# ScalarE instead of VectorE makes the two halves of the scaled incidence matrix, and every queue is ordered anew

## The reference

```python
# layer 0
h = max(layernorm(x), 0)
A_hat = adj + eye; d = A_hat.sum(-1) ** -0.5
x = x + (A_hat * d[:, :, None] * d[:, None, :]) @ (h @ W + b)
# layer 1
h = max(layernorm(x), 0)
H = (adj != 0); w = adj[:, 0, :]              # edge weights: first row of adj
Dn = 1 / (H @ w);  Be = 1 / H.sum(axis=1)     # node and edge degrees
conv(v, W, b) = Dn * (H @ (Be * (H^T @ (v @ W^T)))) + b
g = layernorm(relu(conv(h, W1, b1)), gamma, beta)   # 512 -> 1024
x = x + conv(g, W2, b2) + h                         # 1024 -> 512
```

## Time and profile before

| | |
|---|---|
| median of 3 runs | 1917.77 us |
| profiled execution, its own time | 1915.19 us |
| its span | 1913.3 us |
| TensorE busy | 1881.8 us, 98% |
| VectorE busy | 1661.5 us, 87% |
| ScalarE busy | 1450.5 us, 76% |
| GpSimd busy | 1235.0 us, 65% |
| mean granted TensorE clock | 0.998 |

### The profile page before, as it was taken

The page is one execution under the profiler, slowest core; times in us unless marked ns, Lnnn a source line. Parts: engine busy times, 40 slices in busy tenths (PEclk is TensorE's granted clock), DMA queues, the critical chain, the costliest instruction groups (busy, mean ns, idle before and its releaser), DMA issues.

```text
span 1913.3 us, 37357 instructions
## 1 busy us (share of the span) xinstructions
PE 1881.8 (98%) x10104; PEld 911.1 (48%) x10104; DVE 1661.5 (87%) x3177; ACT 1450.5 (76%) x2726; POOL 1235.0 (65%) x1554
## 2 busy tenths in 40 slices
...
GB/s 231 58 105 96 108 115 90 106 116 84 108 112 90 108 115 90 108 113 91 108 112 91 107 112 91 108 111 90 111 103 98 111 103 99 111 95 99 83 66 78
DMA packets 518736, 197.65 MB, mean 103 GB/s; under 512 B 466816, under 2 KB 483328, under 8 KB 518528
## 3 DMA queue, kind: packets, MB, share of 16 engines
...
...
## 4 chain that ended last, share of the span: by engine, by line
PE 84%; issue 4%; DVE 4%; POOL 2%; DMA 1%; SPq 0%; ACT 0%; DVEq 0%; POOLq 0%
PE ps_u L405 31%; PE ps_e L405 15%; PE ps_x L416 15%; PE ps_z L416 7%; PE ps_y L416 4%; PE ps_y L456 1%; PE ps_y L458 1%; PE ps_y L457 1%; PE ps_t L393 1%; PE ps_t L394 1%; PE ps_t L395 1%; PE ps_e L456 1%; PE ps_e L458 1%; PE ps_e L457 1%; DMA raw_t<-bet_wide 1%
## 5 line engine op out<-in xcount | busy, mean ns | idle before, releaser
L405 PE MATMUL ps_u<-w2h,raw_t 128*128 128x512 f16 x2016 | 476.2, 379 | 0.0
L1506 POOL TENSOR_TENSOR base<-b_all,xh 128x512 f32<-128x512 f32 x128 | 210.9, 1647 | 353.7 <-DVE raw_w L1141 343.8
L405 PEld LDWEIGHTS ps_u<-w2h,raw_t 128*128 128x128 f16 x2016 | 194.6, 98 | 224.3 <-issue 0.8
L1083 DVE SCALAR_TENSOR_TENSOR raw_w<-ps_x,dn,b_all 128x512 f32<-128x512 f32 x192 | 141.9, 739 | 117.3 <-PE ps_x L416 116.9
L405 PE MATMUL ps_u<-w2l,raw_t 128*128 128x512 f16 x1008 | 238.1, 379 | 0.0
L788 ACT ACTIVATE bet_wide<-raw_w 128x1024 f16<-128x1024 f32 x128 | 134.2, 1048 | 78.8 <-DMA raw_t<-bet_wide 75.3
L1498 POOL TENSOR_TENSOR b_all<-x,b_all 128x512 f32<-128x512 f32 x128 | 167.0, 1305 | 16.7 <-DMA b_all<-in_b_dram 7.7
L1556 POOL TENSOR_SCALAR u<-ssq 128x2 f32<-128x2 f32 x64 | 34.1, 532 | 216.9 <-ACT raw_w L773 216.4
L1511 POOL TENSOR_TENSOR base<-base,raw_w 128x512 f32<-128x512 f32 x128 | 166.8, 1303 | 8.0
L779 ACT ACTIVATE raw_w<-raw_w,nm,sc 128x1024 f32<-128x1024 f32 x128 | 151.9, 1232 | 23.3 <-POOL nm L1582 23.3
L1127 DVE TENSOR_TENSOR bet_wide<-raw_w,bet_wide 128x1024 f16<-128x1024 f32 x128 | 158.7, 1240 | 7.2 <-ACT bet_wide L788 3.6
(11 more groups left out here) (178 smaller groups left out, 4901.3 us busy)
## 6 DMA issues: line engine op xcount, KB each, us to landing
x_t<-in_x_dram SPq DMA_DIRECT2D x128, 256.0 KB, 2.9
out_dram<-raw_w SPq DMA_DIRECT2D x128, 256.0 KB, 2.5
...
raw_t<-bet_wide SPq DMA_TRANSPOSE x256, 3.3
...
h0T_hi<-h_hi SPq DMA_TRANSPOSE x128, 2.5
h0T_lo<-h_lo SPq DMA_TRANSPOSE x128, 2.4
...
```

What stands on the lines that cost most here:

```text
L405: mm = pe.matmul(ps, t[:, j * 128:(j + 1) * 128], w[:, j, :], start=(n == 0 and j == 0), stop=(n == 2 and j == blocks - 1))
L1083: return dve.scalar_tensor_tensor(out=z, in0=bank[:, :], scalar=dn1[:, p % 2, j:j + 1], in1=z if row is None else row[:, cols], op0=ALU.mu ...
L1506: pool.tensor_tensor(base[:, g % 6, :], x1b[:, :], xh[:, g % 2, :], ALU.add).then_inc(s_scr2, 1)
```

## The change

`do_HB_hi` and `do_HB_lo` move from VectorE's queue to ScalarE's. The low half was (H^T x inv) - HB_hi before; now the factor itself is split, `inv_hi = f16(inv)` by ScalarE (`do_invh`) and `inv_lo = inv - inv_hi` by VectorE (`do_invl`), and HB_lo = H^T x inv_lo. `inv_lo` is written into `cm`, `inv_hi` into a spare column of HB. Two semaphores are new, and `do_P` waits for both halves. All five queues are ordered anew: the loop takes two pairs a turn and covers pairs 16 to 51, the fillers are 208 in eleven places in place of 178 in eight, and in the start the weights come in another order.

```diff
-    STEADY_FROM, STEADY_TO = 4, NP - 16
+    STEADY_FROM, STEADY_TO = 16, NP - 12
+        inv_hi, inv_lo = HB[:, 0, :, :, N + 1], cm
@@ SyncE's queue
-            do_ldX(0); do_ldX(1)
+            do_ldX(0); do_ldX(1); do_trA(0)
...
-            do_ldX(2); do_ldX(3); do_ldA(4)
+            do_ldA(3); do_ldX(2); do_ldX(3); do_ldA(4); do_ldA(5); do_trA(2)
             load_weight(1, raw_w1, W1T, range(0, 2))
             load_weight(1, raw_w1, W1T, range(2, 4))
-            do_trA(2); do_tr0h(0); do_tr0h(1); do_ldA(5); do_tr0l(0); do_tr0l(1); do_ldA(6)
+            do_tr0h(0); do_tr0h(1); do_tr0l(0); do_tr0l(1); do_ldA(6); do_ldA(7)
@@ TensorE's queue, start
             def do_P(p):
+                pe.wait_ge(s_hbh, 2 * p + 2)
                 pe.wait_ge(s_hbl, 2 * p + 2)
...
-            keep_busy(14, ps_u)
+            keep_busy(13, ps_u)
             gram_of_weight(0, raw_w0, range(0, 4))
-            keep_busy(18, ps_u)
+            keep_busy(37, ps_u)
             weight_sum(0, gram[:, 0, 0:N + 1])
-            keep_busy(60, ps_x)
+            keep_busy(42, ps_x)
             do_P(0)
+            keep_busy(7, ps_x)
             gram_of_weight(1, raw_w1, range(0, 4))
+            keep_busy(20, ps_x)
+            do_P(1)
+            keep_busy(4, ps_x)
+            weight_sum(1, gram[:, 1, 0:N])
             do_Y0(0); do_Y0(1)
+            beta_row(range(0, 2))
+            beta_row(range(2, 4))
+            do_Z0(0)
+            beta_row(range(4, 6))
+            beta_row(range(6, 8))
             do_Z0(1); do_Y0(2)
             weight_sum(2, wsq[:, 0:KH])
+            do_Y0(3); do_Z0(2)
+            keep_busy(27, ps_x)
+            do_Z0(3)
+            keep_busy(9, ps_x)
+            do_P(2); do_Y0(4); do_T1(0)
+            keep_busy(23, ps_x)
+            do_T1(1); do_Z0(4)
+            keep_busy(7, ps_x)
+            do_Y0(5); do_T1(2)
+            keep_busy(19, ps_x)
+            do_M1(0); do_M2(0); do_Z0(5); do_P(3); do_M6(0); do_M5(0); do_M7(0); do_T1(3); do_Y0(6); do_M3(0)
@@ TensorE's queue, loop
-            for k in range(STEADY_FROM, STEADY_TO):
-                do_M1(k); do_Y0(2 * k + 5); do_U(2 * k - 3); do_M6(k); do_Y2(2 * k - 4); do_P(k+2); do_T1(2 * k + 2)
-                do_M7(k); do_Z0(2 * k + 5); do_M5(k); do_Y0(2 * k + 6); do_Y2(2 * k - 3); do_M3(k); do_M4(k)
-                do_M2(k); do_T1(2 * k + 3); do_U(2 * k - 2); do_Z0(2 * k + 6)
+            for k in range(STEADY_FROM, STEADY_TO, 2):
+                do_M1(k); do_Z0(2 * k + 6); do_T1(2 * k + 2); do_P(k+2); do_M2(k); do_Y0(2 * k + 7); do_M6(k)
+                do_U(2 * k - 3); do_M7(k); do_Y2(2 * k - 4); do_Z0(2 * k + 7); do_M5(k); do_Y2(2 * k - 3)
+                do_T1(2 * k + 3); do_M3(k); do_M4(k); do_Y0(2 * k + 8); do_U(2 * k - 2); do_M1(k+1)
...
@@ ScalarE
+            def do_HB_hi(g):
+                p, j = g // 2, g % 2
+                act.wait_ge(s_bi, p + 1)
+                done(act, s_p, p - 1)
+                act.activation(HB_hi[:, p % 2, j, 0:N], A_HT[:, p % 3, j, 2, :], ACT.Copy, scale=inv_t[:, p % 2, j:j + 1])\
+                   .then_inc(s_hbh, 1)
+            def do_HB_lo(g):
...
+                act.wait_ge(s_bil, p + 1)
+                act.wait_ge(s_cnt, g + 1)
+                act.activation(HB_lo[:, p % 2, j, 0:N], A_HT[:, p % 3, j, 2, :], ACT.Copy, scale=inv_lo[:, p % 2, j:j + 1])\
+                   .then_inc(s_hbl, 1)
+            def do_invh(p):
+                m = p % 2
+                act.wait_ge(s_bi, p + 1)
+                done(act, s_bil, p - 1)
+                act.activation(inv_hi[:, m, :], inv_t[:, m, :], ACT.Copy).then_inc(s_bih, 1)
@@ VectorE
+            def do_invl(p):
+                m = p % 2
+                dve.wait_ge(s_bih, p + 1)
                 done(dve, s_hbl, 2 * p - 2)
+                dve.tensor_tensor(inv_lo[:, m, :], inv_t[:, m, :], inv_hi[:, m, :], ALU.subtract).then_inc(s_bil, 1)
@@ VectorE's queue, start: weight 1 is measured ahead of yv(0), and split ahead of x1(1)
+            gram_diagonal(1)
+            weight_magnitude(1)
             split_lo(0, raw_w0, w0h, w0l, range(3, 4))
+            do_w(3); do_h0_lo(2); do_dm(1); do_h0_lo(3); do_ri(1); do_P_lo(1); do_yv(0); do_dn(1); do_cm(2)
             weight_scale(1)
+            do_yv(1); do_yl(0)
             split_lo_w1(range(0, 1))
...
             split_lo_w1(range(4, 5))
+            do_yl(1); do_x1(0)
             split_lo_w1(range(5, 6))
+            do_x1(1); do_inv(2); do_st1(0); do_st1(1); do_yv(2)
```

More of the change, by code:

```diff
@@ L333, in _ @@
             load_weight(2, raw_w2, W2T, range(3, 4))
+            load_weight(2, raw_w2, W2T, range(4, 5))
             load_row(b2_all, b2, s_rows)
-            load_weight(2, raw_w2, W2T, range(4, 5))
             load_weight(2, raw_w2, W2T, range(5, 6))
@@ new lines, in _ @@
+            do_out(NG - 26); do_ul(NG - 25); do_hn_lo(NG - 23); do_out(NG - 25); do_dm(NP - 9); do_P_lo(NP - 9)
+            do_ri(NP - 9); do_z5(NP - 11); do_x1(NG - 15); do_z2(NP - 11); do_z7(NP - 11); do_st1(NG - 15)
+            do_z3(NP - 11); do_w(NP - 7); do_cm(NP - 7); do_aggr1(NG - 15); do_dn(NP - 9); do_inv(NP - 7)
+            do_yv(NG - 14); do_w(NP - 6); do_Hu(NP - 4); do_bn0(NG - 11); do_yl(NG - 14); do_z4(NP - 11)
+            do_aggr0(NG - 11); do_A_lo(NP - 4); do_u0(NP - 6); do_xh_lo(NP - 9); do_tlA(NP - 10); do_Hu(NP - 3)
@@ new lines, in _ @@
+            do_hn_lo(NG - 20); do_yv(NG - 11); do_z6(NP - 9); do_out(NG - 22); do_yl(NG - 11); do_ul(NG - 21)
+            do_z5(NP - 9); do_w(NP - 5); do_z7(NP - 9); do_out(NG - 21); do_dm(NP - 7); do_P_lo(NP - 7)
+            do_ri(NP - 7); do_z3(NP - 9); do_dn(NP - 7); do_x1(NG - 11); do_st1(NG - 11); do_z4(NP - 9)
+            do_aggr1(NG - 11); do_A_lo(NP - 2); do_Hu(NP - 2); do_yv(NG - 10); do_hn_lo(NG - 19); do_z2(NP - 9)
+            do_yl(NG - 10); do_bn0(NG - 7); do_ahat(NP - 1); do_aggr0(NG - 7); do_u0(NP - 4); do_tlA(NP - 8)
@@ new lines, in _ @@
+            do_h0_lo(NG - 6); do_bn0(NG - 4); do_yv(NG - 7); do_z6(NP - 7); do_aggr0(NG - 4); do_h0_lo(NG - 5)
+            do_hn_lo(NG - 16); do_yl(NG - 7); do_invl(NP - 3); do_ul(NG - 17); do_out(NG - 18); do_z5(NP - 7)
+            do_out(NG - 17); do_z7(NP - 7); do_x1(NG - 7); do_dm(NP - 5); do_z3(NP - 7); do_st1(NG - 7)
+            do_z4(NP - 7); do_ri(NP - 5); do_hn_lo(NG - 15); do_P_lo(NP - 5); do_bn0(NG - 3); do_yv(NG - 6)
+            do_aggr0(NG - 3); do_aggr1(NG - 7); do_dn(NP - 5); do_nmu(NP - 7); do_u0(NP - 2); do_tlA(NP - 6)
```

1086 lines of the change are left out of this document (580 added, 506 removed).

## The result

The kernel after takes **1944.01 us** (median of 4 runs, 1941.28 to 1947.04) against 1917.55 us for the kernel before in the same session: ratio 1.0138, 95% interval 1.0125 to 1.0151. It is slower by 26.5 us. The profiled execution took 1943.99 us by its own time, with a span of 1942.2 us.

What follows compares the result with a forecast made beforehand. It took TensorE to bound the loop at 28.76 us a turn and mainly VectorE's list the start; start -0.5, after M1(0) -3.5, loop -1.3, end 0 gave 1917.8 - 5.3 = 1912.5 us, range 1906.5 to 1921.

Steps and rivals of the forecast that it cites:

- The loop: Loop turns: TensorE stays the bound at 28.76 us; half of 2.6 us of x1 waits won, -1.3 (bounds +-2.6).
- x1 before Y0: Loop turn: x1 ends on VectorE at 3.5 us, Y0 wants it at 4.14; a margin of 0.6 us.
- z7 before M4: Loop turn: z7 ends on VectorE at 19.3 us, M4 wants it at 19.7; a margin of 0.4 us.
- Its cover is ScalarE's free time: Loop: ScalarE's added HB work is hidden in its idle time; without that each turn grows by up to 1.4 us.
- HB's own cost: Per pair: VectorE loses 1.2 us and gets 0.15 back; ScalarE gains 1.4, with the two-column copy taken as 0.2.
- The start up to M1(0): Start: 58.0 us of TensorE work plus 14.3 of waits, M1(0) at 72.3; 0.5 us won at equal work, +-4.4.
- Y0(4) for its transposes: Start: TensorE waits 3.4 us at Y0(4) for transposes behind transfers that wait for x1(3).
- this case: Start: granted clock below 1 in more than one stretch, 1.6 us for each 4 us at 0.59; would make the prediction wrong.
- From M1(0) to 112 us: After M1(0): VectorE's list 3.5 us shorter, so TensorE waits 3.5 us less; bounds 0 and 7.1.
- B: Rival: 30 more fillers, 3.3 us, swallow the gain in the start; -2.0, about 1915.8 us; chance 0.29 with its neighbours.
- C: Rival: in the loop M4 waits 0.2 us a turn for z7, 9.6 us over 48 turns, 1922; slower side's chance 0.21.
- The end: Last 14 steps of TensorE: the same as before, 0 us, +-1.

Runs made afterwards that it cites:

- e3: Kernel after with GpSimd's sums and both do_bias0 earlier in its turn, and VectorE's do_dds moved: 1920.02 us, ratio 1.0012.
- e8: Kernel after plus one useless 128x256 ScalarE copy in each loop turn, ahead of do_hn: 1959.97 us, ratio 1.0223.
- e11: Kernel after with HB kept on ScalarE but its operations, and VectorE's do_invl, at other places in the loop: 1926.5 us, ratio 1.005.
- e2: Kernel before with only HB moved to ScalarE and do_invl on VectorE, all other orders as before: 1919.42 us, ratio 1.0009.
- e6: Kernel before with HB on ScalarE only for pairs made in the loop, start and end untouched: 1915.24 us, ratio 0.9992.
- e4: Kernel after with only VectorE's do_dds moved to the middle of the next turn: 1943.68 us, ratio 1.0137.
- e5: e3 with 17 of the 23 fillers ahead of T1(1) left out: 1918.36 us, ratio 1.0007.
- e1: Kernel after, new orders kept, with HB's halves back on VectorE directly behind the reciprocal in do_inv: 1967.27 us, ratio 1.0258.
- e7: As e1, but do_inv with HB stands behind do_xh_lo at the end of VectorE's turn: 1932.14 us, ratio 1.0076.

## Why the prediction was wrong

**The step that failed** is "*The loop.* TensorE has the same matmuls a turn, so 28.76". It tested the new order at TensorE's door: x1 before Y0 (0.6 us) and z7 before M4 (0.4 us). Those margins do hold, in e3, with the same order of TensorE and ScalarE. What it did not do is follow a chain once around: from an instruction through other engines' queues back to the same instruction a turn later. The sum of that ring, 29.84 us in the turn shown, is longer than TensorE's 28.76 and so is the bound. It was to be had roughly beforehand from the new queues and the durations of before: GpSimd's whole turn, 19.0 us by the earlier trace rows, ScalarE's list from `do_h0_hi` to `do_hn_hi`, VectorE's from hn_lo to out; with the 8.2 and 2.6 us of these, 29.8. Which operation of it would be stretched was not: the `do_bias0` rows of before are all near 0.27 us in the loop, and the 1.08 more in 23 turns are what lifts the ring over 28.76. The term was -1.3 (bounds +-2.6); it was +22.7. "Its cover is ScalarE's free time" failed with it: a share of 79% says nothing about an instruction whose neighbours are a ring. e8 puts 0.31 us a turn on 0.41 us of added work there, and e11 gets 17.5 us back by moving HB alone. HB's work is not the cause by itself: with it, e2 and e6 keep turns of 28.76, and so does e3, where GpSimd's bias leaves the ring.

**HB's own cost** was right. VectorE's turn fell by 1.15 us (25.69 to 24.54 in e6; forecast 1.1). ScalarE's rose by 1.37, the mean of 20 turns from 500 us (445.0 us busy before, 472.4 in e6; forecast 1.4); the one turn in the windows shown gives only 0.80, since single turns differ. An HB row takes 0.39 us and not 0.3, but the next starts 0.3 us after it. The two-column copy takes 0.20 us, as taken. The Trainium skill, "VectorE: DVE Perf Modes", the section on the TRN2 errata, gave an estimate of 188 ns, and the trace agrees (0.193 to 0.212). In the order of before the loop is 3.5 us shorter with the move in e6's trace, more than the 1.3 of the prediction.

**The start up to M1(0)** was forecast at 72.3 and came at 78.7. TensorE in order of time, ScalarE's wait that answers to the earlier trace rows, and the windows with the granted clock:

```profile
21.06 0.22 PE L486 MATMUL ps_p<-HB,A_HT 128*128 128x129 f16 x1 [2.19 <-ACT HB L842]
...
25.26 1.89 PE L445 MATMUL ps_z<-raw_w 128*128 128x128 bf16 x16 [1.41 <-DMA raw_w<-in_W1T_dram]
...
64.07 1.89 PE L422 MATMUL ps_e<-w0h,h0T_lo 128*128 128x512 f16 x4 [3.65 <-DMA h0T_lo<-h_lo]
...
67.03 4.10 PE L570 MATMUL ps_x<-ones_wide 128*128 128x256 f16 x23
...
78.72 0.59 PE L433 MATMUL ps_x<-w1h,th 128*128 128x512 f16 x2
```

```profile
19.23 0.31 ACT L706 ACTIVATE A_H<-adj_t 128x128 f16<-128x128 f32 x1 [1.23 <-DMA A_HT<-A_H]
```

```profile
19.00:25.00 6.00, 2.79 (x27) 2.47 (x27) 4.80 (x10) 5.76 (x21) 3.39 (x5) 0.76 1.14 340
25.00:28.00 3.00, 2.74 (x21) 2.44 (x22) 3.00 (x5) 1.74 (x6) 2.53 (x1) 0.50 1.26 215
28.00:36.00 8.00, 7.80 (x48) 4.50 (x46) 7.35 (x18) 6.14 (x17) 5.96 (x4) 0.94 1.02 333
...
64.00:72.00 8.00, 7.93 (x53) 5.75 (x54) 4.55 (x13) 3.36 (x8) 6.33 (x7) 0.63 0.07 18
```

Single waits were forecast more or less well: Y0(4) for its transposes 3.4, measured 3.65; P(0) 1.4, measured 2.19; W1 3.5, measured 1.41; ScalarE's transpose wait fell from 3.15 to 1.23, not to nothing. Their sum was not too small: up to 78.72 us TensorE is idle 13.8, where the forecast had 16.4 with the first wait, and busy 64.9, where it had 55.9. So the same work took longer, and the granted clock says where. Behind P(0)'s and W1's waits it is 0.76 and 0.50, behind Y0(4)'s it is 0.63 for 8 us, where before had 0.99 to 1.00 in all four windows. (Before had 0.59 from 36 to 40 us instead, 1.6 us by the same reckoning, which is gone.) Length times what is missing of the clock: 1.4 + 1.5 + 0.5 + 3.0 = 6.4 us, an upper value, since TensorE is partly idle in the first. That this equals 78.7 - 72.3 is in part luck: six more traces have the same start, e3, e4 and e8 to e11, with M1(0) between 76.3 and 80.1 us; in e3 and e11 the same four windows miss only 3.4 and 3.3 us of clock, and M1(0) comes at 78.6 and 76.3. So the clock accounts for a part of the 6.4 us, and how large a part isn't settled. The text named this case as one that would make it wrong (1.6 us for each such stretch) and put none of it into the sum.

**From M1(0) to 112 us** the term of -3.5 was right. At M1(0) the kernel is 5.9 us later at equal work (9.8 less the 3.9 of work), at w = 140 2.65: 3.2 us won. From 69 to 112 us VectorE works 37.35 us in place of 42.57 and TensorE idles 3.8 in place of 7.1, but that window begins ahead of M1(0) now. With the start 6.4 late, -4.0 becomes +2.4; measured at 140 us of work: +2.7.

**The rivals.** B may be right in kind, and is small: e5 gets 1 to 1.7 us, not resolved. C named the kind of loss that came, a small wait each turn, at the wrong place; its price of 0.2 us a turn was a third of the real one (22.3 us over 36 turns, 0.62). The end, 0 +-1, was +1.4.

**Still open:** the turns of 28.76 amid the longer ones are ones with the short `do_bias0`, but what makes it miss `do_tlS` in these turns, and why the meeting comes in 23 of 36 turns here, in 34 in e1 and in none in e7, isn't known. Nor was it tried whether moving `do_bias0` or `do_tlS` alone brings the loop back to 28.76.
